# Cross-attention and quantised feed-forward on one core: the order of work in the last feed-forward block

## What is computed

```python
def act_quant(x):
    scale = 127.0 / jnp.clip(jnp.max(jnp.abs(x), axis=-1, keepdims=True), 1e-05)
    return jnp.clip(jnp.round(x * scale), -128, 127) / scale

h = bit_linear(x, w1)                      # 256 -> 1024
h = depthwise_conv1d(h.transpose(0, 2, 1), conv_w, conv_b)   # 3 taps over the rows
h = jax.nn.silu(h.transpose(0, 2, 1))
return bit_linear(h, w2)                   # 1024 -> 256, act_quant(h) inside

x = x + _L0_ffn_ref(_layernorm(x, axis=-1), w1, conv_w, conv_b, w2)
```

## Time and profile before

| | us |
|---|---|
| median of three runs | 429.03 (428.88 to 429.48) |
| the profiled execution, its own time | 430.1 |
| its span | 428.3 |
| TensorE matmuls busy | 406.1 (95%) |
| VectorE busy | 375.5 (88%) |
| ScalarE busy | 314.7 (73%) |
| GpSimd busy | 81.8 (19%) |
| end of the last result, from the span's start | 424.91 |

### The profile page before, as it was taken

One profiled execution on the slowest core, in us unless ns is written; L12 is line 12 of the kernel. 1 busy time (PEld: TensorE's weight loads), 2 busy tenths in 40 slices (PEclk: granted clock), 3 DMA queues, 4 the chain that ended last, 5 costly groups with the idle time before them and its releaser, 6 DMA issues.

```text
span 428.3 us, 14055 instructions
## 1 busy us (share of the span) xinstructions
PE 406.1 (95%) x6035; PEld 279.8 (65%) x6035; DVE 375.5 (88%) x595; ACT 314.7 (73%) x369; POOL 81.8 (19%) x109
## 2 busy tenths in 40 slices
PE   6999998999899999999999999999999998999885
PEld 6666675676567666666676666666676665676673
DVE  5889988988887899899799799799789899999994
ACT  2466777798979667766766767766766689999984
POOL 3387776101100020020020020020020010221200
PEclk9999999999999999999999999999999999999999
DMA  7825367112112112111111111111111000001002
GB/s 223 227 27 107 54 107 177 53 48 67 40 39 73 43 39 64 40 51 63 40 40 58 57 40 38 64 51 40 41 38 40 2 2 0 2 27 49 26 26 80
DMA packets 28687, 24.62 MB, mean 57 GB/s; under 512 B 6278, under 2 KB 28367, under 8 KB 28623
## 3 DMA queue, kind: packets, MB, share of 16 engines
q1 hardware_dynamic: 26106, 21.59, 15.7%
q0 software_dynamic: 2176, 2.10, 4.1%
q10 hardware_dynamic: 340, 0.01, 0.0%
HBM read 9.00 MB, written 2.10 MB: 26 GB/s over the span
## 4 chain that ended last, share of the span: by engine, by line
PE 49%; DVE 29%; ACT 16%; issue 4%; POOL 1%; DMA 1%; ACTq 0%; DVEq 0%
DVE arena L732 17%; PE sc L1742 11%; PE heads L1759 5%; ACT arena L1321 5%; PE heads L1760 4%; PE heads L1761 4%; PE heads L1567 3%; PE sc L1579 3%; ACT qq L1412 3%; PE by L1646 2%; ACT qq L1420 2%; PE sc L1846 2%; PE bx L1579 2%; PE by L1579 2%; ACT arena L1334 1%
## 5 line engine op out<-in xcount | busy, mean ns | idle before, releaser
L732 DVE SCALAR_TENSOR_TENSOR arena<-arena 128x1024 bf16<-128x1024 f32 x160 | 190.7, 1220 | 28.4 <-ACT arena L1321 27.3
L1321 ACT ACTIVATE arena<-sc,kb 128x1024 f32<-128x1024 f32 x160 | 170.0, 1114 | 58.0 <-PE sc L1742 57.9
L1759 PEld LDWEIGHTS heads<-v,arena 128*128 128x128 bf16 x1280 | 117.1, 97 | 40.3 <-issue 27.2
L1759 PE MATMUL heads<-v,arena 128*128 128x65 f16 x1280 | 129.7, 194 | 3.7 <-DVE arena L732 3.1
L1760 PE MATMUL heads<-v,arena 128*128 128x64 f16 x1280 | 128.9, 195 | 0.0
L1761 PE MATMUL heads<-v,arena 128*128 128x65 f16 x1280 | 128.3, 192 | 0.0
L1742 PE MATMUL sc<-qs,kst 64*128 64x512 f16 x960 | 118.0, 378 | 1.6 <-ACT arena L1321 0.9
L1760 PEld LDWEIGHTS heads<-v,arena 128*128 128x128 bf16 x1280 | 118.7, 97 | 0.1
L1761 PEld LDWEIGHTS heads<-v,arena 128*128 128x128 bf16 x1280 | 118.7, 99 | 0.0
L1742 PEld LDWEIGHTS sc<-qs,kst 64*128 64x128 f16 x960 | 40.1, 94 | 46.7 <-issue 3.5
L534 POOL TENSOR_SCALAR frs<-fmv 128x2 f32<-128x2 f32 x8 | 8.0, 996 | 221.2 <-DVE fmv L806 221.2
(11 more groups left out here) (209 smaller groups left out, 587.1 us busy)
## 6 DMA issues: line engine op xcount, KB each, us to landing
kst<-kk SPq DMA_DIRECT2D x80, 128.0 KB, 2.0
xs<-in_x SPq DMA_DIRECT2D x8, 256.0 KB, 5.2
xs<-in_L_xattn_b_out POOLq DMA_DIRECT2D x8, 256.0 KB, 6.0
qs<-qq SPq DMA_DIRECT2D x16, 128.0 KB, 2.4
out<-cbuf SPq DMA_DIRECT2D x7, 256.0 KB, 2.1
xs<-in_ctx SPq DMA_DIRECT2D x6, 256.0 KB, 6.1
xs<-in_L_ffn_w SPq DMA_DIRECT2D x1, 1024.0 KB, 6.0
cbuf<-in_L_ffn_w SPq DMA_DIRECT2D x1, 1024.0 KB, 9.2
```

Of the source, the lines that this page charges most:

```text
L732: e.scalar_tensor_tensor(out=rest[:, j, :, :], in0=prob[:, j, :, :], scalar=SHRINK, in1=probh[:, j, :, :], op0=ALU.mult, op1=ALU.subtract) ...
L1321: a_.activation(prob[:, j, :, :], sc[(j + 1) % 2][:, :, :], ACT.Exp, bias=kb[:, bass.ds(i * QUAD + j, 1)]).then_inc(exp_done[j], 1)
L1759: t_.matmul(o, hi, row[:, 0:OW], start=first and sub == 0, stop=False, skip_group_check=True)
```

## The change

Five edits in the last block:

- On TensorE the order of the last block's transposes and products is another one. Second f32 transposes come directly after the first, the third ones before the f16 transposes of tile 3.0, the product of 3.1 after all transposes.
- On VectorE and ScalarE the largest values, results and whole numbers are reordered, and the whole numbers of tile 3.1 move from ScalarE to VectorE (`by_dve`).
- The product bank alternates from tile 2.3 on (`SPREAD` is 10), before only within block 3; a product waits for the result two before it.
- The whole numbers of tile 3.3 are written to `dq16` instead of `uq[1]`, and no longer wait for the product of 3.1.
- From tile 2.3 on VectorE's scale also waits for GpSimd's `scale_back` of the tile four before, which read the same slot.

```diff
+        SPREAD = NF * FT - FT - 2
         def product_bank(n, t):
-            return ob[t % 2 if n == NF - 1 else 0]
+            return ob[max(0, n * FT + t - SPREAD) % 2]
-        by_dve = [(NF - 2) * FT + 3, (NF - 1) * FT + 2]
+        by_dve = [(NF - 2) * FT + 3, (NF - 1) * FT + 1, (NF - 1) * FT + 2]
+        def whole_of(m):
+            return dq16[:, :, :, :].rearrange("p w t d -> p (w t d)") if m == NF * FT - 1 else uq[m % 2]
...
# VectorE, largest(n, t)
                 dve.wait_ge(s["scale_step"], steps_before(m) + 1)
+                dve.wait_ge(s["scale_back"], m - FT + 1)
...
# VectorE, feed_forward
                 largest(3, 0)
                 whole(2, 3)
+                largest(3, 1)
                 result(2, 2)
-                largest(3, 1)
                 largest(3, 2)
+                largest(3, 3)
+                whole(3, 1)
                 result(2, 3)
-                largest(3, 3)
+                whole(3, 2)
                 result(3, 0)
-                whole(3, 2)
                 result(3, 1)
                 result(3, 2)
                 result(3, 3)
...
# ScalarE, whole(n, t)
-                wait(act, "o_ps", m - 1)
-                a_.activation(uq[t % 2], ...
+                if m < NF * FT - 1:
+                    wait(act, "o_ps", m - 1)
+                a_.activation(whole_of(m), ...
# ScalarE, feed_forward
                 whole(3, 0)
                 quantize(3, 1)
-                whole(3, 1)
                 quantize(3, 2)
...
# TensorE, second_product(n, t)
-                wait(pe, "res_ready", m - (n == NF - 1 and t > 0))
+                if m <= SPREAD:
+                    wait(pe, "res_ready", m)
+                elif m >= SPREAD + 2:
+                    pe.wait_ge(s["res_ready"], m - 1)
...
# TensorE, feed_forward
                 tokens_first(3, 0)
+                tokens_first(3, 1)
+                hidden_first(2, 3)
                 second_product(2, 2)
-                hidden_first(2, 3)
-                tokens_first(3, 1)
+                tokens_first(3, 2)
                 hidden_first(3, 0)
-                tokens_first(3, 2)
                 second_product(2, 3)
                 tokens_first(3, 3)
                 hidden_first(3, 1)
                 second_product(3, 0)
-                second_product(3, 1)
                 hidden_first(3, 2)
                 hidden_first(3, 3)
+                second_product(3, 1)
                 second_product(3, 2)
                 second_product(3, 3)
```

More of the change, by code:

```diff
@@ L239, in xattn_ffn @@
             rstd2_ready dq_ready xd_ps xd_ready h_ps edge_ps center_ready left_ready taps_done edge_step edge_done
-            u_ready row_step ut_ps scale_step scale_pool scale_back uscale_ready uscale_late uf_ready uqt_ps uq_ready uq_late0 uq_late1 o_ps res_ready pad_done passed""".split()
+            u_ready row_step ut_ps scale_step scale_pool scale_back uscale_ready uscale_late uf_ready uqt_ps uq_ready uq_late0 uq_late1 uq_late2 o_ps res_ready pad_done passed""".split()
         s = {n: sem(n) for n in names}
@@ L1418, in whole @@
                 act.wait_ge(s["uqt_ps"], m + 1)
-                wait(act, "o_ps", m - 1)
-                a_.activation(uq[t % 2], uqt[turned(n, t)], ACT.Identity, bias=shifts[:, 1:2]).then_inc(s["uq_ready"], 1)
+                if m < NF * FT - 1:
+                    wait(act, "o_ps", m - 1)
+                a_.activation(whole_of(m), uqt[turned(n, t)], ACT.Identity, bias=shifts[:, 1:2]).then_inc(s["uq_ready"], 1)
             def late_heads_t(i):
@@ L1902, in second_product @@
                 for j in range(J):
-                    last = t_.matmul(product_bank(n, t), uq[t % 2][:, j * P:(j + 1) * P], w2t[:, j, :], start=(j == 0), stop=(j == J - 1))
+                    last = t_.matmul(product_bank(n, t), whole_of(m)[:, j * P:(j + 1) * P], w2t[:, j, :], start=(j == 0), stop=(j == J - 1))
                 last.then_inc(s["o_ps"], 1)
```

## The result

The changed kernel takes 429.96 us, the median of 19 runs (429.20 to 430.75), against 429.00 us for the kernel before (19 runs): a ratio of 1.002, 95% interval 1.0014 to 1.0026 (0.6 to 1.1 us). The forecast was 428.6, the range 428.1 to 429.2. The profiled execution of the changed kernel took 430.73 us, its span 428.9; that of the kernel before 430.1 and 428.3. What lies around the span is the same (1.8 us), so the loss is inside it.

A forecast was written before the change was run, and what follows sets the result against it. No engine is full in the tail, so order and waits were taken to bound it. A gain of 0.82 us, less 0.36 given back, left 0.46 off the 429.03 median: 428.6 us, range 428.1 to 429.2.

The forecast's parts named there:

- Steps 1 to 5: Last block: earlier f32 transposes and freed ScalarE gain 0.82 us, 0.36 given back before the last product; sum 0.46 us.
- The added wait before the scale: VectorE's wait for scale_back after each of five largest values: 0.04 us, counted once on the path, in largest 3.3.
- 3.4 us of a store that every version pays: Behind the last result, to the span's end: 3.4 us of store, taken as the same in every version.
- step 6: Last stores: a later pair store and closer last stores cost 0, with 0.2 us either way.
- B: Slower: the store of tiles 2.2 and 2.3 lands late and holds up result 3.2; 430.7 us, chance 0.05.
- C: Slower: TensorE falls to half clock after idling from 419.62 to 420.64; 431.7 us, chance 0.02.
- A: More than 0.86 us faster: shorter releases, free added wait, last store 0.2 quicker; 428.1 us, chance 0.14.
- D: Nothing gained: tile 3.0's f16 transposes come later than 414.76; 429.0 us, chance 0.77 together with the forecast.
- an unforeseen slower course: No place named: the remaining chance of 0.02 for a slower result.
- the chance of slower (0.09): Whole kernel slower by over 0.2%: B, C and the unforeseen rest together, chance 0.09.

The follow-up runs named there:

- e13: Changed kernel without the path for other masks, plus 24 semaphore increments early in VectorE's program: 429.18 us, ratio 0.9993 to the kernel before.
- e9: Changed kernel plus 24 early VectorE semaphore increments and 218 memsets at the head of VectorE's untaken path: 429.45 us, ratio 1.0009 to the kernel before.
- e11: Kernel before plus 7 early VectorE semaphore increments and 121 memsets at the head of VectorE's untaken path: 430.02 us, ratio 1.0024.
- e7: Kernel before with VectorE's program lengthened by five scale_back waits and two one-column fills, order unchanged: 430.28 us, ratio 1.0036.
- e3: Kernel before with the store of tiles 3.0 and 3.1 also waiting for result 3.2: 429.59 us, ratio 1.0012.
- e6: Kernel before without the path for other masks on VectorE, ScalarE and TensorE: 428.33 us, ratio 0.9988.
- e2: Changed kernel with the store of tile 3.2 issued from ScalarE's queue: 429.99 us, ratio 1.0023 to the kernel before.
- e4: Changed kernel with TensorE and ScalarE held at their ends until the last result is written: 430.24 us, ratio 1.0028 to the kernel before.
- e10: Changed kernel plus 242 memsets at the head of VectorE's untaken path alone: 430.27 us, ratio 1.0030 to the kernel before.
- e18: Changed kernel with 48 semaphore increments ahead of TensorE's first instruction, VectorE's boundary unmoved: 434.77 us.
- e1: Changed kernel with its last two tiles in one store: 429.78 us, ratio 1.0018 to the kernel before.
- e5: Changed kernel without the path for other masks on VectorE, ScalarE and TensorE: 429.45 us, ratio 1.0011 to the kernel before.
- e17: e9 plus 48 semaphore increments ahead of TensorE's first instruction and 208 at the head of its untaken path: 433.85 us.
- e14: Changed kernel with the two paths exchanged in memory on three engines, so the taken one lies last: 433.74 us.
- e15: Kernel before with the two paths exchanged in memory on three engines, so the taken one lies last: 435.04 us.
- e8: Changed kernel with all four computing engines held until the last store has landed: 432.35 us, ratio 1.0074 to the kernel before.

## Why the prediction was wrong

**Steps 1 to 5 held.** Against F3.0's start, which came 0.31 earlier: F3.2 413.93 (predicted 413.89), Q3.0 414.83 (414.76), F3.3 416.74 (416.63), largest 3.3 417.84 (417.70), quantisation 3.3 419.48 (419.38), Q3.3 420.74 (420.64), S3.3 422.96 (422.84), result 3.3 424.09 to 424.57 (423.97 to 424.45). The one shortfall is 0.11 us at F3.3, whose release from ScalarE took 0.15 instead of 0.11 (415.17 + 1.11 to 416.43) behind a whole-number pass that itself ran 0.07 late; it carries through to the end, so the gain is 0.34 and not 0.46. The added wait before the scale, taken as 0.04, cost at most 0.01 (largest to scale 1.26 in the earlier trace rows, 1.26 here).

**The step that failed is the one that was not a step:** "From the last result to the span's end are 3.4 us of a store that every version pays". It was read from one profile as a constant. In the versions that leave the taken path by a branch ahead of the last landing it is 2.18 us of a store and its end, and 0.9 to 2.5 us on top that come with the fetching of code. Their size depends on two things that this change moves: how many instructions VectorE has, and when the stores stand against the exit. In the profiled executions the 3.37 became 4.65. With it failed the pricing of step 6, "I take 0, with 0.2 either way": its reasoning about the data of the stores overlapping each other was right (e13 shows none), but the rival traffic was not on the list.

**The sum as it came:** −0.34 for the order. VectorE's block boundary costs 0.5 (after against e9), 1.0 (e11 against before) or 1.4 (e7 against before). The stores brought closer to the exit fetches cost the rest, 0.8 by difference (e9's 429.45 less the 428.66 that the order alone would give); e3, which brings only the pair's store closer, in the kernel before, shows 0.6, with an interval that starts at 0. −0.34 + 0.5 + 0.8 is the 0.96 measured because the 0.8 was taken as the remainder: the sum is no check of its terms. With e7's 1.4 for the boundary nothing would be left for the stores. The added waits, costed by their 0.04 us of time, were dear by their place in memory.

**Rivals.** B named the stores as the place of a loss, but the wrong one: result 3.2 never waited. C: the clock stayed at 1.00. A and D didn't come. The 0.02 left for "an unforeseen slower course" is where the result lies, and the chance of slower (0.09) was too small for a tail of which 3.4 us had been taken as given without asking what is in them. The page cited on DMA latency (the Trainium skill, DMA: Bandwidth & Descriptors) would have put the loss in a store at high load; these stores were slow with the DMA engines idle most of the time (busy share 0.27 from 424.26 to 428.90 in the kernel after, 0.18 behind the last result of the kernel before).

**How the trace compares with the page on code.** The Trainium skill (Runtime: NRT & Kernel Launch, Instruction fetch mechanics) says that each engine's sequencer fetches its next block of code by a DMA queue of its own, mostly hidden, and that a taken branch beyond the blocks at hand forces a fetch. The trace agrees that blocks come in step with the code (58 ahead of the tail of the kernel after) and that the exit branches are followed by fetches. What the 58 cost was not measured, so that they are mostly hidden rests on the page. The trace shows only two queues of code, though, and VectorE's and ScalarE's blocks come on the same one. That the hidden kind can cost 1 us where it falls beside the last store is what e11 adds.

**What stays open.** How a fetch slows a store was not isolated. In the trace of the kernel after, 14 of the last pair's 16 completion packets end within 0.15 us of each other and the store lands 2.7 us after them, and 24 of the 626 data packets of 1 KB in the last stores take 120 to 520 ns, where nearly all take 46 and none in e6 and e13 takes more. That fits one or two DMA engines being shared; no run separated it from another cause. Nor is the late store the only thing that is late. The span ends when all engines have met, and in eight traces (before, after, e2, e4, e7, e10, e11, e18) the last to arrive is VectorE, whose last instruction starts 0.35 to 0.39 us behind the landing. Had the store of the kernel after landed at once, VectorE's own exit, which ends at 4.42, would still have held the end there unless it depends on the same thing. In e1, with the boundary at the same place, VectorE is done at 3.60 and the store, landing at 4.05, alone holds the end. What ties the two, and which of them the block at the boundary delays first, isn't shown; e5, where VectorE is done at -0.09 and one fetch still goes with a landing of 2.3 instead of 1.7, shows the store alone, in one execution. The split of 0.5 and 0.8 is open too, as e11 puts 1.0 and e7 1.4 on the boundary. No version that keeps both paths was found faster than the kernel before: e9, with the new order and the boundary moved, is at 429.45. e6, which drops the path for other masks, is 0.5 us faster than the kernel before (interval 0.1 to 0.9), with the same order.

## What to carry to other kernels

Before taking the time behind the last result as fixed, ask what is in it: with no code fetched beside it the span ended 2.18 us after the last result here, and everything beyond that came only where code was fetched. When a small change to the order near a kernel's end comes out slower although every block moved as planned, compare the fetches of code and the landings of the last stores first, and try a few harmless instructions far away from the end: if seven of them in the first 2.1 us move the time by 1 us, the code's position is what is measured. Look whether the place is free: VectorE's first microseconds were (e9, e11), TensorE's were not (e17, e18).

## What the runs showed of the hardware that was not expected

- Seven semaphore increments on VectorE in the first 2.1 us, 21 ns each, made a kernel of 429 us 1.0 us slower (e11). They added one 8 KB block of code, fetched 1.4 us after the last result, and the tail grew from 3.37 to 4.14.
- A 128 KB store lands 1.7 us after its issue with no code fetch beside it (e6, e13, e14, e15), 2.7 to 2.9 with the exit fetches of the kernel before, 3.8 in the kernel after; a 256 KB store 2.1, 2.6 and 4.5.
- The branches out of the taken path over the unused one cost about 4 us with nothing beside them (e8, from 426.4 to 430.5), and 4 to 6 us where they are placed at the path's entry (e14 4.6, e15 5.9 above the kernel before).
- Without code fetches every completion packet of a store ends within 0.2 us of the others and no 1 KB packet takes over 46 ns (e6, e13).
